# First attention of a two-layer gated block: TensorE's order around the two turns of probabilities in even slots

## The reference

```python
# scores: 16 heads of 32 channels, q from the normalised x, k = v = ctx
scores = einsum('bhqd,bhkd->bhqk', qh, kh) / sqrt(32)
scores = where(ki <= qi + (Sk - Sq), scores, -10000)   # Sq 112, Sk 375
out = einsum('bhqk,bhkd->bhqd', softmax(scores), vh)
x = x + tanh(g_xattn[0]) * out
```

## Time and profile before

| what | value |
| --- | --- |
| three runs | 2052.89, 2053.58, 2054.22 us |
| span of the profiled execution | 2052.6 us |
| TensorE busy in it | 1996.6 us, 97% |
| VectorE, ScalarE, GpSimd busy | 1240.7, 1158.7, 850.5 us |
| DMA | 33% of 16 engines, 210.08 MB |
| mean granted TensorE clock | 0.991 |

### The profile page before, as it was taken

One profiled execution on the slowest core, in us unless ns is written; L12 is line 12 of the kernel. 1 busy time (PEld: TensorE's weight loads), 2 busy tenths in 40 slices (PEclk: granted clock), 3 DMA queues, 4 the chain that ended last, 5 costly groups with the idle time before them and its releaser, 6 DMA issues. The chain is left out here.

```text
span 2052.6 us, 37477 instructions
## 1 busy us (share of the span) xinstructions
PE 1996.6 (97%) x13369; PEld 1675.6 (82%) x13369; DVE 1240.7 (60%) x2332; ACT 1158.7 (56%) x3064; POOL 850.5 (41%) x1013
## 2 busy tenths in 40 slices
PE   8999999999999999999989997899999999999998
PEld 6877777777778888898868886799999999878886
DVE  6766666666645644464445555666666666566665
ACT  5666666666643333353433445877777777455554
POOL 3525536346324100000003444888888878122222
PEclk9999999999999999999999998999999999999999
DMA  6435436354355210203003335333333342421001
GB/s 186 146 103 177 135 112 220 119 154 142 115 185 204 83 67 1 72 1 118 1 26 103 123 114 157 85 90 109 107 98 105 100 115 85 124 70 48 28 28 37
DMA packets 193272, 210.08 MB, mean 102 GB/s; under 512 B 59533, under 2 KB 133757, under 8 KB 192589
## 3 DMA queue, kind: packets, MB, share of 16 engines
q1 hardware_dynamic: 193101, 207.83, 33.0%
HBM read 128.13 MB, written 79.66 MB: 101 GB/s over the span
## 5 line engine op out<-in xcount | busy, mean ns | idle before, releaser
L1874 POOL TENSOR_TENSOR qd_rows<-qd_rows,c_rsum 112x375 f32<-112x375 f32 x256 | 202.2, 811 | 85.9 <-DVE c_rsum L2004 78.6
L2010 DVE TENSOR_TENSOR c_pT_lo<-c_turned,c_pT_hi 125x336 fp32r<-125x336 f32 x256 | 128.6, 503 | 130.9 <-ACT c_pT_hi L1949 130.8
L1940 ACT ACTIVATE qd_rows<-c_score,c_nmax 112x375 f32<-112x375 f32 x256 | 147.0, 574 | 87.1 <-DVE c_nmax L1999 87.1
L1305 ACT ACTIVATE b_silu<-b_gate,ab_scales 128x512 f32<-128x512 f32 (+1 forms) x64 | 40.6, 635 | 254.2 <-PE b_up L1434 254.2
L1371 DVE SCALAR_TENSOR_TENSOR b_hidden<-b_up,ab_scales,b_silu 128x512 f32<-128x512 f32 (+1 forms) x64 | 43.7, 684 | 196.6 <-ACT b_silu L1305 196.6
L2299 POOL TENSOR_TENSOR f_probs<-f_probs,f_rsum 112x448 f32<-112x448 f32 x64 | 59.7, 933 | 211.6 <-DVE f_rsum L2425 211.6
L531 ACT ACTIVATE a_probs<-a_score,a_nmax 112x375 f32<-112x375 f32 x256 | 144.5, 575 | 2.6 <-DVE a_nmax L700 2.6
L953 PEld LDWEIGHTS a_turned<-keep_ident,a_probs 112*125 112x125 f32 x768 | 110.9, 189 | 35.5 <-issue 22.5
L1999 DVE TENSOR_REDUCE c_nmax<-c_score 112x1 f32<-112x375 f32 x256 | 137.6, 538 | 0.6 <-PE c_score L2080 0.6
L953 PE MATMUL a_turned<-keep_ident,a_probs 112*125 112x112 f32 x768 | 134.5, 284 | 1.0 <-DVE a_pT L706 0.7
L1283 POOL TENSOR_TENSOR ab_zT<-ab_zT,keep_ln_eps 128x1 f32<-128x1 f32 x1 | 0.2, 189 | 298.7 <-DVE ab_zT L1405 298.7
(11 more groups left out here) (353 smaller groups left out, 6098.6 us busy)
## 6 DMA issues: line engine op xcount, KB each, us to landing
q<-q_qT SPq DMA_DIRECT2D x14, 1024.0 KB
qd_raws<-q SPq DMA_DIRECT2D x64, 224.0 KB, 4.1
k<-bq_raw SPq DMA_DIRECT2D x16, 752.0 KB, 4.1
qd_raws<-k SPq DMA_DIRECT2D x64, 188.0 KB, 2.9
v<-bq_raw SPq DMA_DIRECT2D x48, 250.0 KB
qd_raws<-v SPq DMA_DIRECT2D x64, 187.5 KB
bq_raw<-in_ctx_dram SPq DMA_DIRECT2D x15, 672.0 KB
wug<-a_ug_turned SPq DMA_DIRECT2D x32, 256.0 KB, 2.3
```

The source lines that it names most:

```text
L1874: pool.tensor_tensor(probs[:, n % AHEAD, :], probs[:, n % AHEAD, :], rsum[:, n % (2 * H):n % (2 * H) + 1].broadcast_to([S, T]), ALU.mult). ...
L1940: act.activation(probs[:, n % AHEAD, :], score[n % AHEAD][0:S, 0:T], ACT.Exp, bias=nmax[:, c:c + 1], accum_out=sums[:, c:c + 1]).then_inc( ...
L2010: dve.tensor_tensor(pT[1][:, t % 2, :, j, :], src, f32(pT[0][:, t % 2, :, j, :]), ALU.subtract).then_inc(pT_split, 1)
```

## The change

Only the order of calls in TensorE's loop changes. In even slots `weigh` moves ahead of the slot's first turn, directly behind the scores. The second turn of every slot moves behind the half projections of slots 2, 4 and 6 and behind the keys' turn of slot 0. Odd slots keep their order, since nothing of theirs lies between the old and the new place of the second turn. The programs of the other engines, the buffers and the waits inside the functions are the same.

```diff
@@ -1017,16 +1017,16 @@
                             scores(b, n // 2 + 1)
                         elif after:
                             scores(b + 1, 0)
+                    if n == 0 and before:
+                        weigh(b - 1, G - 1)
+                    if n in (2, 4, 6) and cur:
+                        weigh(b, n // 2 - 1)
                     if cur:
                         turn_probs(b, n, 0)
-                    if n == 0 and before:
-                        weigh(b - 1, G - 1)
                     if n == 0 and b == B:
 
                         pe.wait_ge(ab["scales_loaded"], 48)
                         pe.transpose(turned[:, 0:3 * IC], scale_rows[:, :], ident[0:3 * IC, 0:3 * IC]).then_inc(scales_turned, 1)
-                    if n in (2, 4, 6) and cur:
-                        weigh(b, n // 2 - 1)
                     if n == 0 and after:
                         turn_ctx(b + 1, 0)
                     if n == 1 and before:
@@ -1045,8 +1045,6 @@
                         rotate_z(b - 2)
                     if n == 7 and cur:
                         project(b, "v", 2, 0)
-                    if cur:
-                        turn_probs(b, n, 1)
                     if n == 2 and cur:
                         project(b, "v", 0, 1)
                     if n == 4 and cur:
@@ -1055,6 +1053,8 @@
                         project(b, "k", 2, 1)
                     if n == 0 and before:
                         turn_keys(b - 1, 2)
+                    if cur:
+                        turn_probs(b, n, 1)
                     if n == 0 and before and cur:
                         project(b, "k", 0, 0)
                     if n == 1 and cur:
```

## The result

The changed kernel takes 2077.41 us (median of four runs, 2077.09 to 2078.98) beside 2053.79 for the kernel before, run beside it: 23.6 us slower, ratio 1.0116 with a 95% interval of 1.0103 to 1.0129. The profiled execution took 2078.98 us with a span of 2077.3. I forecast 2075.6 us, 22.0 slower, in a range of 2060 to 2085.

What follows compares the result with a forecast made beforehand. TensorE's distances between starts bound the kernel; slots 2, 4, 6 and 0 add 0.05 + 0.43 + 0.47 + 0.42 = 1.37 us a batch, times 16 = 21.9, with edges +22.5, taken as +22: 2075.6 us, range 2060 to 2085.

Steps and rivals of the forecast that it cites:

- The bound: TensorE, first attention: busy 99.9 of 100 us, so the stage's time is the sum of distances between its starts.
- The gain of 0.20 us a slot: Even slots: first turn (F) behind weighted sums (W) 0.35 not 0.51, second turn (L) 0.31: 0.20 us saved per slot.
- rival A: Only the stop between array shapes counts, waits on copies would not show: 10 us faster, 2043.5 us; chance 0.06.
- VectorE's copy in slots 2, 4 and 6: Second turn (L) to next slot's first (F') needs 1.17 us; F' 4.41, 4.56, 5.41 behind scores (S).
- W's wait for the job's copy: Slots 4 and 6: weighted sums (W) need the job's bank copied, so start 0.86 us behind scores instead of 0.71.
- The keys behind the sums' copy in slot 0: Keys' turns wait for ScalarE's copy of the sums in their bank, starting at 2.78 instead of 2.20; slot +0.42 us.
- Slot 6: Sums 0.86, first turn 1.58, rotation 1.93, half projection 2.78, second turn 4.24, next slot's first turn 5.41 against 4.94: +0.47.
- The edges: First batch lacks keys in slot 0: -0.4; last lacks four turns (X) in slots 2, 4 and next context: +0.6, +0.4.
- What is late next: VectorE's second maximum, ScalarE's exponentials, next scores: slot 4's second turn 1.46 us later, 2.27 free, so it stays hidden.
- B: Only VectorE's copy is waited for; sums' bank free in time in slots 0, 4, 6: +8 us, 2061.5; chance 0.13.
- C: Scores to weighted sums costs a stop of its own, 0.20 us more: 8 us on top, 2083.6; chance 0.10.
- D: Stops saved and waits added cancel, needing waits of 0.16 us a slot: no change, 2053.6 us; chance 0.05.

Runs made afterwards that it cites:

- the earlier job: Changed kernel with the job of slots 3 and 5 ahead of the last two matmuls of its half projection: 2073.09 us, ratio 1.0091.
- the fastest version: Changed kernel with half projection cut around second turn in slots 2 and 4, second turn behind rotation in slot 6, slot 0 reordered, job earlier: 2048.03 us.

## Why the prediction was right

*The bound.* Right: TensorE's starts carried the sum. All other programs were unchanged, and every slot's length followed from the order and from three round trips through a copy.

*The gain of 0.20 us a slot.* Right in kind and in slots 2 and 4, where F lasts 0.35 and L 0.31; alone, with the waits out, it showed as 0.14 to 0.17 a slot (2048.03 us). In slots 0 and 6 it was too high: in front of the context turns and of the rotation F lasts 0.41 and 0.42 (204.05 to 204.46, 231.92 to 232.34), not 0.35. In slot 0 the wait for the sums' copy covers that. The rule that a change of tiling mode drains TensorE (the Trainium skill, "TensorEngine Tiling (Array Packing)", Tiling Modes) agrees with the trace in one place: F in front of W costs 0.51, behind W 0.35. But no cost of its own shows between S and W, though both are tiled differently (0.70, against 0.71 in front of a turn). Taken alone for the whole change, the rule gives the wrong sign, as in rival A.

*VectorE's copy in slots 2, 4 and 6.* Right to 0.01 us at F' in slots 2 and 4 (4.41 and 4.56), and shown from both sides: cut away, it returned 17.5 us; doubled, it cost 19.7 us more, for 19 to 20 expected. What was mis-sized is what follows: TensorE's first turn after a wait takes longer to its successor, 0.39 and 0.32 (216.41 to 216.80, 225.87 to 226.19) where I took 0.31 and 0.26. The changed kernel's trace has these distances, within 0.01, behind every such wait but the first, at 21.20 us. So slot 2 came out at +0.10, not +0.05, and slot 4 at +0.54, not +0.43; of slot 4's 0.11, this explains 0.06, and the rest is spread over rows of slot 5 and has no cause shown.

*W's wait for the job's copy.* 0.84 instead of 0.86; worth 4.3 us in all, shown by the earlier job.

*The keys behind the sums' copy in slot 0.* 2.78 as forecast; worth 8.3 us.

*Slot 6.* 0.10 too high at F', although F cost 0.07 more than I took. The rotation takes 0.85 in front of a turn, and I kept that. In front of the projection it takes 0.42 and the projection 1.74 instead of 1.47 (232.34, 232.76, 234.50): 2.16 for the two, not 2.31.

*The edges* went as computed in kind: in the last batch F' of slots 3 and 5 stands without X, with 0.69 us idle in front of it each time, and the pair of slot 2 grew by 0.73, for 0.65. What I left out there is slot 0: without the next context turns the keys wait longer, and its pair grew by 0.61 instead of 0.42. *What is late next*: nothing in the scores' chain, as said, even with L another 0.4 us later.

*The rivals.* A (2043.5) names a real gain, but it needed F' 0.73 behind L, and it stands 1.16 behind it; B and C are excluded by the slots' rows, since all three waits are there and S to W has no stop of its own; D needed waits of 0.16 a slot.

The sum was 1.37 us a batch; 1.50 was measured. The four slots missed by +0.02, +0.05, +0.11 and -0.05, so errors of both signs stand in it: the restarts after the three waits on VectorE's copy add 0.08, 0.06 and 0.07, and slot 6 takes 0.10 back. That the total of 22.0 lies so near to 23.6 is in part luck. From the scores of slot 2 of the first batch on, the new order cost 24.7 us in the traces; the start of the trace, which no term of the prediction is about, was 1.3 us earlier (26.84 against 28.11). The term of 0.72 for W in front of a turn was also read 0.01 too high (206.72 to 207.43).

## What to carry to other kernels

When two users of one PSUM bank alternate with copies by other engines, write down the shortest distance for each hand-over (here 1.17 us from turn to turn through VectorE, 1.12 through ScalarE, 1.35 from a turn to a bank behind two copies of ScalarE) and keep that much of TensorE's own work between them; a reordering that saves a change of array shape is only worth making if every such distance stays covered. Work that can be cut (a projection of twelve matmuls) is the filler: four matmuls on one side and two on the other took 17.5 of the 23.6 us back, and with slot 0 and the jobs of slots 3 and 5 cut in likewise, and L moved behind the rotation in slot 6, the loss became a gain of 6.2. And before a piece is moved earlier or later, list what queues behind its copy on the copying engine: that is where the wait turns up again.

## What the runs showed of the hardware that I had not expected

A group of three transposes that TensorE starts after having waited takes 0.06 to 0.08 us more to the next group than such a group in a running stream (0.39 against 0.31, 0.32 against 0.26). A full-precision product of 448 columns costs 0.42 us in front of a projection that then takes 0.27 more, so 0.69 in all; in front of a turn it costs 0.77 behind a turn (in the fastest version) and 0.85 behind the weighted sums, so its price depends on its neighbours. And the list of waits names the releaser only for the part of a wait that the modelled end of the matmuls ahead leaves open: of the 0.43 us lost in front of F' in slot 3, 0.26 has VectorE's name, and of the 0.14 in front of W none has ScalarE's; both are also in the "issue" of the weight loads.
